# Macaron block on one NeuronCore: attention operands in 64 rows a head, the mask in the operands, eight heads per value bank

## The reference

```python
q = (x @ Wq + bq).reshape(Bb, Ss, H, HD)     # k, v alike
scores = jnp.einsum('bthd,bshd->bhts', q, k) / jnp.sqrt(HD)
scores = jnp.where(causal, -jnp.inf, scores + alibi)
attn = jax.nn.softmax(scores, axis=-1)
out = jnp.einsum('bhts,bshd->bthd', attn, v).reshape(Bb, Ss, Dd)
return out @ Wo + bo
```

## Time and profile before

| | |
|---|---|
| median of 3 runs | 1056.23 us (1055.88 to 1057.18) |
| profiled execution, its own time | 1056.2 us |
| its span | 1056.2 us, mean granted TensorE clock 0.965 |
| share of the span busy | PE 90%, DVE 73%, ACT 63%, POOL 57% |
| DMA | 64.50 MB in all, 22.8% of 16 engines |

### The profile page before, as it was taken

The page is one execution under the profiler, slowest core; times in us unless marked ns, Lnnn a source line. Parts: engine busy times, 40 slices in busy tenths (PEclk is TensorE's granted clock), DMA queues, the critical chain, the costliest instruction groups (busy, mean ns, idle before and its releaser), DMA issues. The chain is left out here.

```text
span 1056.2 us, 26705 instructions
## 1 busy us (share of the span) xinstructions
PE 954.3 (90%) x6880; PEld 501.3 (47%) x6880; DVE 776.1 (73%) x2596; ACT 660.2 (63%) x1570; POOL 603.5 (57%) x1220
## 2 busy tenths in 40 slices
PE   5999993689999989989998998999999996899997
PEld 2444441345555545455554554554555543444443
DVE  5999983677677767767876876776677732799996
ACT  4767763146676746657666675675666674577675
POOL 3777775236646635556464563654646343477777
PEclk9999996799999989999999998999999999899999
DMA  6500001434223223141231421323224001010011
GB/s 170 129 0 0 0 0 44 112 86 121 66 57 103 78 66 91 36 117 53 70 91 47 107 76 48 91 63 90 78 45 112 11 1 22 11 31 21 29 30 40
DMA packets 78828, 64.50 MB, mean 61 GB/s; under 512 B 9818, under 2 KB 78426, under 8 KB 78426
## 3 DMA queue, kind: packets, MB, share of 16 engines
q1 hardware_dynamic: 78734, 63.19, 22.8%
HBM read 33.54 MB, written 29.36 MB: 60 GB/s over the span
## 5 line engine op out<-in xcount | busy, mean ns | idle before, releaser
L1062 DVE TENSOR_REDUCE att_neg_max<-att_max 128x1 bf16<-128x384 f32 (+3 forms) x704 | 424.1, 640 | 164.0 <-PE att_max L865 163.8
L960 ACT ACTIVATE att_probs<-att_exp 128x512 f32<-128x512 f32 x640 | 358.7, 598 | 224.8 <-PE att_exp L883 223.7
L1026 POOL TENSOR_SCALAR_AFFINE_SELECT att_probs<-att_probs 128x256 f32<-128x256 f32 (+1 forms) x640 | 229.9, 363 | 314.3 <-ACT att_probs L960 306.3
L862 PE MATMUL att_max<-att_k_st,att_q_st 114*128 114x128 bf16 (+3 forms) x1024 | 278.5, 310 | 34.2 <-DMA att_k_st<-qk_parts 15.7
L883 PE MATMUL att_exp<-att_q_st,att_k_st 116*128 116x256 bf16 (+3 forms) x1024 | 245.6, 303 | 1.1 <-ACT att_probs L960 1.0
L865 PE MATMUL att_max<-bf_consts 128*128 128x128 bf16 x1024 | 200.3, 225 | 0.0
L862 PEld LDWEIGHTS att_max<-att_k_st,att_q_st 114*128 114x128 bf16 x1024 | 101.1, 99 | 202.9 <-issue 84.6
L900 PE MATMUL att_pv<-att_probs,att_v 128*32 128x512 f32 (+3 forms) x2048 | 191.6, 446 | 1.2 <-POOL att_probs L1026 1.2
L344 ACT ACTIVATE moe_scaled<-moe_hi,moe_gates 128x128 f32<-128x128 f32 x512 | 146.1, 372 | 59.3 <-PE moe_hi L290 58.9
L504 DVE SCALAR_TENSOR_TENSOR x<-moe_lo,moe_gates,x 128x128 f32 (+1 forms) x512 | 160.5, 338 | 18.9 <-PE moe_lo L284 17.9
L284 PE MATMUL moe_lo<-moe_we,moe_hT 128*128 128x512 f32 x256 | 135.1, 610 | 0.0
(11 more groups left out here) (77 smaller groups left out, 923.1 us busy)
## 6 DMA issues: line engine op xcount, KB each, us to landing
qk_parts<-att_parts SPq DMA_DIRECT2D x192, 128.0 KB, 2.3
att_q_st<-qk_parts SPq DMA_DIRECT2D x32, 384.0 KB, 3.9
att_k_st<-qk_parts SPq DMA_DIRECT2D x64, 192.0 KB, 4.3
x<-in_L_attn_x SPq DMA_DIRECT2D x16, 256.0 KB, 3.0
out<-x SPq DMA_DIRECT2D x16, 256.0 KB, 2.3
att_k_st<-zero_rows SPq DMA_DIRECT2D x4, 384.0 KB
moe_we<-in_L_ffn_We SPq DMA_DIRECT2D x2, 512.0 KB, 4.3
att_q_st<-att_shift SPq DMA_DIRECT2D x64, 4.0 KB, 2.9
```

The lines of the kernel that those rows point to most:

```text
L862: nc.tensor.matmul(max_ps[m % RING][:, c * width:(c + 1) * width], q_st[par][0:MAX_K, r, i * P:(i + 1) * P], k_st[par][ab][0:MAX_K, r, 0:w ...
L960: nc.scalar.activation(probs[g % 2][:, n, :], exp_ps[m % RING][:], ACT.Exp).then_inc(exp_done, 1)
L1026: nc.gpsimd.affine_select(out=view, in_=view, compare_op=ALU.is_ge, fill=0.0, base=0, pattern=[[0, len(blocks)], [1, P]], channel_multipli ...
L1062: nc.vector.tensor_reduce(neg_max[par][:, g // 2, ab:ab + n_ab, r0:r0 + n_r, i].rearrange("p a r -> p r a"), max_ps[m % RING][:, 0:len(hea ...
```

## The change

- **Operands.** A head has 64 rows: 48 rows of parts, 3 of ALiBi, 11 "fine" mask rows, one "far" row, one shift row. Head ab = 0 of a pair stands in partitions 0 to 63, head ab = 1 in 64 to 127. There is one `q_st` a sequence, and two k operands, `k_max` (fine rows, for the max pass) and `k_exp` (far row and shift row, for the exp pass). Zero rows are gone. The reload of a half is 6 DMAs of 192 KB rather than 3 (384, 192 and 192 KB).
- **Max pass.** The matmul with `future_b` is gone. A unit has one matmul of 51 rows over the columns left of the diagonal block, if there are any, and one of 62 rows over the diagonal block, where the products of the fine rows lower the future keys. The value found can differ from the row's maximum; as a shift it cancels in the softmax. The wide units come first.
- **Groups.** Group g takes side ab = g % 2 of the four pairs of half g // 2, in both passes, so that both passes of a step read the same 64 partitions at a time.
- **Values.** `v` has for each head 32 columns, of which side 0 uses the first 16 and side 1 the last 16, the others being zero. Two groups accumulate into one bank: eight heads. So there are two copies to `oT`, two transposes back (`turn_o0`, `turn_o1`), two reciprocals and two multiplications per sequence, of double width. The value matmuls are as many and as wide as before.
- **Mask.** POOL zeroes diagonal blocks in four calls of four blocks a group, after slots 3, 7 (two) and 9, rather than in ten calls of one or two blocks.
- **Biases.** The bias of v is multiplied by Wo once at the start and added to bo; the evacuation of `project_v` is a plain copy.
- **Order.** `SIDE_WORK` and `PREPARE` are laid out anew.

The rest of the diff is declarations, semaphore counts and the constants' placement.

```diff
+ALIBI_ROW = HEAD_ROWS
+FINE_ROW = ALIBI_ROW + 3
+FINE = 12
+FINES = -(-P // FINE)
+FAR_ROW = FINE_ROW + FINES
+SHIFT_ROW = FAR_ROW + 1
+SIDE = 64
+assert SHIFT_ROW + 1 == SIDE
...
+        at = np.arange(S) % P
+        group, within = at // FINE, at % FINE
+        fine = np.arange(FINES)[:, None]
+        k_fine = np.where(group == fine, -(2.0 ** (10 * within)), 0.0)
+        q_fine = np.where(group == fine, 2.0 ** (4 - 10 * within), np.where(group < fine, 2.0 ** 14, 0.0))
+        k_far = -(2.0 ** np.round(0.43 * (np.arange(S) - S // 2) - 15))
+        q_far = 2.0 ** np.round(-0.43 * (np.arange(S) - S // 2) - 15)
...
-    {2: "shift_hi", 5: "turn_o2"},
-    {1: "turn_h", 4: "project_q", 6: "turn_o3", 8: "project_k"},
-    {0: "turn_o", 3: "shift_lo", 5: "turn_o0", 7: "project_v"},
-    {0: "output", 5: "turn_o1"},
+    {2: "shift_hi"},
+    {1: "turn_h", 3: "turn_o1", 5: "project_q", 8: "project_k"},
+    {0: "turn_o", 3: "shift_lo", 6: "project_v"},
+    {1: "output", 3: "turn_o0"},
...
-  (1, 5): "split_q0", (1, 6): "split_q1", (1, 7): "split_q2", (1, 8): "split_q3", (1, 9): "split_k0", (1, 10): "split_k1", (2, 0): "split_k2", (2, 2): "split_k3"
+  (1, 6): "split_q0", (1, 7): "split_q1", (1, 8): "split_q2", (1, 9): "split_q3", (1, 10): "split_k0", (2, 0): "split_k1", (2, 1): "split_k2", (2, 2): "split_k3"
...
 def max_unit(n):
-    return [(0, [0, 1, 2, 3]), (1, [0, 1]), (1, [2, 3]),
-            (2, [0]), (2, [1]), (2, [2]), (2, [3]), (3, [0]), (3, [1]), (3, [2]), (3, [3])][n]
+    return [(3, [0]), (3, [1]), (3, [2]), (3, [3]), (2, [0]), (2, [1]), (2, [2]), (2, [3]),
+            (1, [0, 1]), (1, [2, 3]), (0, [0, 1, 2, 3])][n]
 def exp_unit(n):
-    pair, u = divmod(n, 5)
-    return pair, [[(0, 0, 0)], [(0, 1, 0), (0, 3, 3 * P)], [(0, 2, 0), (1, 2, 2 * P)],
-                  [(1, 0, 0)], [(1, 1, 0), (1, 3, 3 * P)]][u]
+    if n < 4:
+        return [(n, 0, 0)]
+    if n < 8:
+        return [(n - 4, 1, 0), (n - 4, 3, 3 * P)]
+    return [(2 * (n - 8), 2, 0), (2 * (n - 8) + 1, 2, 2 * P)]
...
-                k_st = self.k_st[i][ab]
-                eng.dma_start(k_st[ALIBI_ROW:ALL_K], self.consts.k_rows[ab]).then_inc(self.rows_in, DMA)
-                eng.dma_start(k_st[(1 - ab) * HEAD_ROWS:(2 - ab) * HEAD_ROWS],
-                              self.consts.zero_rows).then_inc(self.rows_in, DMA)
+                r = ab * SIDE
+                eng.dma_start(self.q_st[i][r + ALIBI_ROW:r + SHIFT_ROW], self.consts.q_rows).then_inc(self.rows_in, DMA)
+                eng.dma_start(self.k_max[i][r + ALIBI_ROW:r + FAR_ROW],
+                              self.consts.k_max_rows[ab]).then_inc(self.rows_in, DMA)
+                eng.dma_start(self.k_exp[i][r + ALIBI_ROW:r + SIDE],
+                              self.consts.k_exp_rows[ab]).then_inc(self.rows_in, DMA)
...
-                sp.dma_start(q_st[par][0:2 * HEAD_ROWS, pairs, :],
-                             scratch[par, 0, pairs].rearrange("r u t d s -> (u t d) r s")).then_inc(
-                    stack_in[par][hf], DMA)
-                for ab in range(2):
-                    sp.dma_start(k_st[par][ab][ab * HEAD_ROWS:(ab + 1) * HEAD_ROWS, pairs, :],
-                                 scratch[par, 1, pairs, ab].rearrange("r t d s -> (t d) r s")).then_inc(
-                        stack_in[par][hf], DMA)
+                for side, stacks in ((0, (q_st,)), (1, (k_max, k_exp))):
+                    for dst in stacks:
+                        for ab in range(2):
+                            sp.dma_start(dst[par][ab * SIDE:ab * SIDE + HEAD_ROWS, pairs, :],
+                                         scratch[par, side, pairs, ab].rearrange("r t d s -> (t d) r s")).then_inc(
+                                stack_in[par][hf], DMA)
...
+                half_at, ab = g // 2, g % 2
                 for c, hh in enumerate(heads):
-                    r, ab = divmod(4 * g + hh, 2)
-                    nc.tensor.matmul(max_ps[m % RING][:, c * width:(c + 1) * width],
-                                     q_st[par][0:MAX_K, r, i * P:(i + 1) * P], k_st[par][ab][0:MAX_K, r, 0:width],
-                                     start=True, stop=False)
-                    mm = nc.tensor.matmul(max_ps[m % RING][:, (c + 1) * width - P:(c + 1) * width],
-                                          consts.ident_b, consts.future_b, start=False, stop=True)
+                    r, at, low = 4 * half_at + hh, c * width, ab * SIDE
+                    if i > 0:
+                        nc.tensor.matmul(max_ps[m % RING][:, at:at + width - P],
+                                         q_st[par][low:low + FINE_ROW, r, i * P:(i + 1) * P],
+                                         k_max[par][low:low + FINE_ROW, r, 0:width - P], start=True, stop=True)
+                    mm = nc.tensor.matmul(max_ps[m % RING][:, at + width - P:at + width],
+                                          q_st[par][low:low + FAR_ROW, r, i * P:(i + 1) * P],
+                                          k_max[par][low:low + FAR_ROW, r, width - P:width], start=True, stop=True)
                 mm.then_inc(max_out, 1)
...
+                low = (g % 2) * SIDE
+                for hh, j, c in exp_unit(n):
+                    r = 4 * (g // 2) + hh
                     mm = nc.tensor.matmul(exp_ps[m % RING][:, c:c + S - j * P],
-                                          k_st[par][ab][0:ALL_K, r, j * P:(j + 1) * P],
-                                          q_st[par][0:ALL_K, r, j * P:S], start=True, stop=True)
+                                          k_exp[par][low:low + SIDE, r, j * P:(j + 1) * P],
+                                          q_st[par][low:low + SIDE, r, j * P:S], start=True, stop=True)
                 mm.then_inc(exp_out, 1)
...
+                half_at, ab = divmod(g, 2)
                 if j == 0:
-                    pe.wait_ge(masked, b * NE + (g + 1) * EXP_UNITS)
-                    if g > 0 or after(b, 0):
-                        pe.wait_ge(pv_read, b * GROUPS + g)
+                    pe.wait_ge(masked, b * NK + (g + 1) * MASK_UNITS)
+                    if ab == 0 and (g > 0 or after(b, 0)):
+                        pe.wait_ge(pv_read, b * HALVES + half_at)
                     if g == 0:
                         pe.wait_ge(side_read, use(b - 1, "project_v"))
                 for hh in range(4):
-                    pair, ab = divmod(hh, 2)
-                    n, c = next((n, c) for n in range(EXP_UNITS) for a, jj, c in exp_unit(n)[1]
-                                if exp_unit(n)[0] == pair and (a, jj) == (ab, j))
-                    mm = nc.tensor.matmul(pv_ps[VW * hh:VW * (hh + 1), j * P:S], v[par][:, j, 4 * g + hh, :],
-                                          probs[g % 2][:, n, c:c + S - j * P], start=(j == 0), stop=(j == T - 1))
+                    n, c = next((n, c) for n in range(EXP_UNITS) for h, jj, c in exp_unit(n) if (h, jj) == (hh, j))
+                    mm = nc.tensor.matmul(pv_ps[VW * hh:VW * (hh + 1), j * P:S], v[par][:, j, 4 * half_at + hh, ab, :],
+                                          probs[g % 2][:, n, c:c + S - j * P], start=(ab == 0 and j == 0),
+                                          stop=(ab == 1 and j == T - 1))
                 if j == T - 1:
                     mm.then_inc(pv_out, 1)
...
+            pe.wait_ge(bv_spread, 1)
+            nc.tensor.matmul(side_ps[:, 0:D], bv_cols[:], w["wo"][:], start=True, stop=True).then_inc(bias_out, 1)
+            pe.wait_ge(bias_ready, 1)
...
             def copy_values(b, par, g, j):
-                if j < T - 1:
+                if j < T - 1 or g % 2 == 0:
                     return
+                hf = g // 2
                 act.wait_ge(pv_out, b * GROUPS + (g + 1))
-                if g > 0 or after(b, 0):
...
-                    act.wait_ge(turned, use(b + 1 if g == 3 else b, f"turn_o{(g - 1) % GROUPS}"))
+                if hf == 1:
+                    act.wait_ge(turned, use(b, "turn_o0"))
+                elif after(b, 0):
+                    act.wait_ge(turned, use(b, "turn_o1"))
...
-                pieces = exp_unit(n)[1]
-                view = probs[g % 2][:, n, :].rearrange("p (a c) -> p a c", c=P)
-                blocks = [c // P for _, _, c in pieces]
-                view = view[:, 0:1, :] if len(blocks) == 1 else view[:, 0:blocks[1] + 1:blocks[1], :]
+                if n not in (3, 7, EXP_UNITS - 1):
+                    return
                 pool.wait_ge(exp_done, b * NE + (g * EXP_UNITS + n + 1))
                 pool.sem_inc(pool_passed, 1)
-                nc.gpsimd.affine_select(out=view, in_=view, compare_op=ALU.is_ge, fill=0.0, base=0,
-                                        pattern=[[0, len(blocks)], [1, P]], channel_multiplier=-1).then_inc(masked, 1)
+                group = probs[g % 2][:].rearrange("p n (a c) -> p n a c", c=P)
+                if n == EXP_UNITS - 1:
+                    views = [group[:, 8:10, 0:3:2, :].rearrange("p n a c -> p (n a) c")]
+                else:
```

(28 more changed lines are left out.)

99 lines of the change are left out of this document (49 added, 50 removed).

## The result

The changed kernel is slower: 1095.91 us, median of 4 runs (1094.08 to 1101.76), against 1056.62 us before, with a fourth run. The ratio is 1.0372, interval 1.0328 to 1.0416. The forecast was 1019 us, in a range of 990 to 1045. One run further down is in a slower state, the profiled one of e4 (1026.6 us, 1.6% above e4's fastest): it is left out of e4's time and clock, and only its trace is read.

The account below looks back on a forecast made before the run. PE was taken as bound by columns streamed in attention. Fifteen steps at -2.6 us (-39) and +2.1 us for start and end took 1056.2 us to 1019 us, with a range of 990 to 1045.

Parts of the forecast that it names:

- the sentence on the rows: PE's max matmuls: contracting over 51 and 62 rows rather than 114 counts at nothing, since matmuls go by columns.
- One of my own signs: Attention step with both passes: 38 to 38.5 us expected; under 37 or over 40 us would show the forecast wrong.
- The steps without the clock: Fifteen attention steps with both passes: 2.6 us less each, 39 us in all.
- Mask matmul: Max pass on PE: dropping the mask matmul saves 0.22 us a head, 3.5 us a step for 16 heads.
- transposes: Transposes back on PE: four sets of four become two, saving 0.9 us a step.
- new waits: PE waiting at wide slots and side-bank reads: two pairs of side items at 0.25 us each, +0.5 us a step.
- Switches: PE changing array shape between 64-row passes and side items: 13 at 0.10 us, +1.3 us a step.
- The pause: First max matmul of every second step: five pauses, 14.3 us in all, taken for the loop's and left unchanged.
- The start: Before the attention steps: reload +2.2 us, bias chain +1.2 us; the first max pass alone unchanged.
- The end: Last exp pass loses two copies, -1.2 us; the end after it -0.1 us.
- The values, mask and copies: Work on DVE, ACT and POOL beside PE: counted at nothing; POOL's four-block mask call at most 0.82 us.
- The weight loads' rival: Max and exp matmuls: 64-row weight loads no longer hidden; with the whole 99 ns each, 1280 us; chance 0.07.

Follow-up runs that it names:

- e4: The changed kernel with the max pass on the opposite side of the pairs from the exp pass in each group; 1016.6 us.
- e11: The changed kernel with the max matmul left of the diagonal on 63 rows of q_st and k_exp instead of 51 of q_st and k_max; 1048.3 us.
- e3: The changed kernel with four zero-padded k operands a sequence instead of two, so max and exp matmuls contract over all 128 rows; 996.8 us.
- e5: e3 with max and exp matmuls cut to 66 rows, still full array shape, part of the contraction left out; 1037.5 us.
- e9: e5 with 64 rows for 66, so the 64-row shape with its switches, all on partitions 0 to 63; 1036.5 us.
- e1: The kernel before with max, mask and exp matmuls cut to 66 rows, part of the contraction left out; 1105.4 us.

## Why the prediction was wrong

**The step that failed** is the sentence on the rows: "The rows on which it contracts, 51 and 62 rather than 114, I count at nothing". It is right for the distance between matmuls, as the timeline after shows, and wrong for the clock, which I took as given. The granted clock of the fifteen steps went from 0.98 to 0.83. No rival of mine had it: my way to slower was weight loads that show, and 64-row matmuls of 128 columns follow at 0.06, so they stay hidden. One of my own signs did show it: the two steps above take 40.2 and 48.4 us, over the 40 that I had named.

**What the clock cost.** No step of the changed kernel ran at full clock from end to end, but e11 differs from it only in the rows of one kind of matmul, and its steps at 1.00 take 38.68 us. Fifteen of them are 580 us, where the changed kernel took 662.0: 82 us for the clock. (One minus the clock times the stretch, 0.17 x 662.0, would say 113. It says too much: the step of 48.4 is 9.7 over 38.7, where half of its 23.9 us at half clock would be 12.)

**The steps without the clock** were forecast well. From 41.13 to 38.68 are 2.45 us a step where I had 2.6, so 37 of the 39 us. With the pause gone (14) and some 2 us of clock lost before, 632.8 - 37 - 14 - 2 + 82 gives the 662 measured.

**Mask matmul, transposes and new waits**, -3.5, -0.9 and +0.5 a step: nearly held together. A step of e3 or e5, which have no new switches, takes 37.8 us at full clock, where the forecast says 37.1 (41.0 - 3.5 - 0.9 + 0.5). No run divides the 0.7 between the three.

**Switches**, +1.3 from 13 at 0.10: nearly. 0.09 each by the timeline, 1.1 us a step between e5 and e9, 0.9 between e3 and e11. The net comes out well because two small errors offset one another. The Trainium skill's rule (TensorEngine Tiling (Array Packing), Key Properties), that a change of tiling mode drains, agrees with this 0.09 also for rows.

**The pause** of every second step, which I left in, is gone: 14.3 us in the earlier trace rows, no such line after. It stands in e1 as before (15.2 us in 5), and at the first max matmul in no run made from the changed kernel. Why, no run tried. Those 14 us came to the kernel without a term of mine.

**The start** was under-priced: the first exp matmul comes 8.8 us later (221.8 to 230.6), where I had 3.4 (bias 1.2, reload 2.2). The first reload is issued at 189.39 and the first max matmul starts at 197.60, 8.2 us, against 5.2 in the earlier trace rows: my upper bound of +2.6 was too low. That issue is itself 2.0 us later than before (187.41), where I had 1.2. The six transfers of the other half go out before that matmul too, where there were three; that they slow the first six is my guess, and no run tried it. Then the first max pass takes 33.0 us against 29.16 in the earlier trace rows, at a clock of 0.50, and 33.0 in e3 as well, where a wait of 5.0 us for the second sequence's reload stands before the first exp matmul (22.4 in two waits, 17.4 of them the first):

```profile
PE att_max L894 <- DMA att_k_exp<-qk_parts: 22.4, 2, 17.4
```

**The end** I put at -1.3 us; from the last window's end to the end of the span are 201.6 us before and 202.3 after, +0.7. So the 38.7 us between the spans are 29.2 in the fifteen steps, 8.8 at the start and 0.7 at the end.

**Slips in my sums.** With the switches at 0 the time is 1056.2 - 58.5 + 2.1 = 999.8, and not the 1005 that I gave as the lower end of the forecast's own range. There are 19 steps, -2 to 16, and not 18; nothing rests on that.

**The values, mask and copies** on the other engines, at nothing: held, since PE stayed the bound. The wide forms, as groups of the changed kernel:

```profile
L1064 POOL TENSOR_SCALAR_AFFINE_SELECT att_probs<-att_probs 128x512 f32<-128x512 f32 x256 | 159.8, 637 | 328.2 <-ACT att_probs L992 328.2
L1151 DVE TENSOR_TENSOR att_o<-att_side,att_rden 128x256 f32<-128x256 f32 x32 | 13.6, 424 | 1.1
L1149 DVE RECIPROCAL att_rden<-att_side 128x32 f32<-128x32 f32 x32 | 11.3, 353 | 24.9 <-PE att_side L967 24.7
L1003 ACT ACTIVATE att_oT<-att_pv 128x512 f32<-128x512 f32 x32 | 19.1, 598 | 3.4 <-PE att_pv L928 3.3
```

POOL's call of four blocks takes 0.637 us where I gave 0.82 as the most. The reciprocal of double width takes 0.353, not about the 0.257 of the earlier trace rows.

**The weight loads' rival.** The Trainium skill's rule (TensorE: Matmul & The Clock Gate, What overlaps and what doesn't) is that weight loads overlap with matmuls in flight only on another row group. A load takes 0.10 us here, so by that rule 128-column matmuls on one side would stand at 0.10 and more. They stand at 0.06 at full clock. The trace disagrees.

## What to carry to other kernels

A matmul over half the rows is as fast as one over all, but it may cost PE its clock: where a change narrows the contraction of most matmuls, look at the granted clock first and at distances second. If the clock has fallen with PE busy throughout, try to fill the contraction with rows of zeros; here that was worth 99 us, some 15 of them from the switches of shape that went too, and it cost SBUF only. To price a lost clock, take a step at full clock from a near variant: the mean clock times the stretch overstated it here (113 us against 82). And where nothing hides a reload, let the first reader wait only for what it reads: the first max matmul came 6.6 us after the first issue with four of six transfers awaited, 8.8 with six.
